# Row sums inverted through DRAM, and the value product of a pair's second half in one piece

## The reference

```python
qf = jnp.concatenate([q_nope, q_pe], axis=-1)        # 128 + 64 wide
kf = jnp.concatenate([k_nope, k_pe], axis=-1)
scores = jnp.einsum('bhnd,bhmd->bhnm', qf, kf) * scale
scores = jnp.where(causal, scores, jnp.finfo(scores.dtype).min)
attn = jax.nn.softmax(scores, axis=-1)
out = jnp.einsum('bhnm,bhmd->bhnd', attn, v)
out = out.transpose(0, 2, 1, 3).reshape(b, n, HEADS * VDIM)
return out @ Wout
```

## Time and profile before

| | |
|---|---|
| median of 3 runs | 1745.24 us (1744.07 to 1745.45) |
| span of the profiled execution | 1743.9 us, its mean granted clock 0.996 |
| TensorE busy | 1690.3 us, 97% |
| VectorE busy | 1237.6 us, 71% |
| ScalarE busy | 982.1 us, 56% |
| GpSimd busy | 572.6 us, 33% |
| preparation, attention loop, feed-forward part | to about 70 us, to about 1243 us, to the end |

### The profile page before, as it was taken

One profiled execution on the slowest core, in us unless ns is written; L12 is line 12 of the kernel. 1 busy time (PEld: TensorE's weight loads), 2 busy tenths in 40 slices (PEclk: granted clock), 3 DMA queues, 4 the chain that ended last, 5 costly groups with the idle time before them and its releaser, 6 DMA issues. The chain is left out here.

```text
span 1743.9 us, 32128 instructions
## 1 busy us (share of the span) xinstructions
PE 1690.3 (97%) x11280; PEld 1384.5 (79%) x11280; DVE 1237.6 (71%) x2858; ACT 982.1 (56%) x2319; POOL 572.6 (33%) x498
## 2 busy tenths in 40 slices
PE   5799999999999999999999999999999999999998
PEld 4677777778777777777777777777699999999998
DVE  6878788778788788787887878877654454555543
ACT  6566666666666666666666666666533333433332
POOL 4553344434443344433344334434401110110100
PEclk9899999999999999999999999999999999999999
DMA  8300000012000003000001100001200000000000
GB/s 285 123 7 7 7 14 7 8 30 76 13 8 7 7 7 103 8 7 7 9 12 49 56 7 14 7 7 42 81 1 25 25 1 25 25 13 13 13 13 13
DMA packets 35868, 51.45 MB, mean 30 GB/s; under 512 B 2368, under 2 KB 26944, under 8 KB 35712
## 3 DMA queue, kind: packets, MB, share of 16 engines
q1 hardware_dynamic: 35712, 49.39, 8.7%
HBM read 35.23 MB, written 14.16 MB: 28 GB/s over the span
## 5 line engine op out<-in xcount | busy, mean ns | idle before, releaser
L1296 ACT ACTIVATE probs<-aps,nmax 128x384 f32<-128x384 f32 (+7 forms) x512 | 378.8, 744 | 215.9 <-DVE nmax L1353 210.1
L1353 DVE CUSTOM_DVE_ANT_0 aps<-aps,mask_row 128x384 f32<-128x384 f32 (+7 forms) x512 | 388.6, 770 | 132.0 <-PE aps L43 125.7
L1222 PE MATMUL aps<-ident,probs 128*128 128x128 f32 x2304 | 329.1, 272 | 0.8 <-ACT probs L1296 0.6
L43 PE MATMUL aps<-kTh,qh 128*128 128x512 f32 (+3 forms) x768 | 293.6, 382 | 8.8 <-POOL ql L1452 3.8
L1222 PEld LDWEIGHTS aps<-ident,probs 128*128 128x128 f32 x2304 | 271.8, 140 | 23.3 <-issue 1.4
L1307 ACT COPY pT<-aps 128x512 f32<-128x512 f32 (+3 forms) x485 | 233.8, 506 | 89.1 <-PE aps L1222 86.2
L43 PE MATMUL aps<-pT,v 128*64 128x512 f32 (+3 forms) x1536 | 268.9, 492 | 0.6 <-ACT pT L1307 0.6
L43 PE MATMUL aps<-kTl,qh 128*128 128x512 f32 (+3 forms) x768 | 257.4, 343 | 0.0
L1445 POOL TENSOR_TENSOR rot<-rot 64x512 f32<-64x512 f32 x128 | 163.4, 1277 | 185.8 <-DVE rot L1367 185.8
L43 PEld LDWEIGHTS aps<-pT,v 128*64 128x64 f32 x1536 | 101.7, 136 | 152.1 <-issue 142.1
L43 PE MATMUL aps<-kTh,ql 128*128 128x512 f32 (+3 forms) x768 | 221.7, 343 | 0.0
(11 more groups left out here) (193 smaller groups left out, 3037.4 us busy)
## 6 DMA issues: line engine op xcount, KB each, us to landing
wqs<-wq_scratch SPq DMA_DIRECT2D x30, 256.0 KB, 2.6
raw_numbers<-in_x SPq DMA_DIRECT2D x8, 512.0 KB, 6.6
acc<-in_x SPq DMA_DIRECT2D x8, 512.0 KB, 3.6
x_scratch<-acc SPq DMA_DIRECT2D x8, 512.0 KB, 3.0
x<-x_scratch SPq DMA_DIRECT2D x8, 512.0 KB, 3.9
out<-x SPq DMA_DIRECT2D x7, 512.0 KB, 2.9
heads<-in_heads SPq DMA_DIRECT2D x4, 640.0 KB, 8.2
wout<-in_Wout SPq DMA_DIRECT2D x4, 512.0 KB, 8.8
```

The source lines that it names most:

```text
L43: return nc.tensor.matmul(out, lhsT, rhs, start=start, stop=stop, skip_group_check=True)
L1222: last = nc.tensor.transpose(tps[:, TS.index(x) % 3, j * P:(j + 1) * P], probs[c][:, c * (pair % 2), a, off:off + P], t.ident[:])
L1296: nc.scalar.activation(probs[c][:, c * (r % 2), a, off:off + w], sps[:, at:at + w], ACT.Exp, bias=nmax[:, c, a, j:j + 1], scale=-1.0, accu ...
L1353: nc.vector.tensor_tensor_reduce(out=s, in0=s, in1=mask[:, N - PW[c][j]:N], scale=-1.0, scalar=3.0e38, op0=ALU.add, op1=ALU.min, accum_out ...
```

## The change

The four transposes L(c), the product REP(c) and the copy LOUT(c) go. INV(c) now writes its eight inverses per token into the first of 32 columns and turns them with VectorE's own transpose, which works on blocks of 32x32: inverse m of tokens 32s to 32s + 31 comes to lie on partition 32s + m. `spread_inverses` on SP stores the four blocks to a DRAM scratch of 8 rows of 128 numbers, waits for them, and loads each head's four rows to 64 partitions of `linv_b`. O(c) waits for these two loads.

PV(1, 0, 4) and PV(1, 4, 4) become PV(1, 0, 8) in the place of the second. `pT` has 16 buffers instead of 12, and a block's buffer is counted on through the bodies. All other jobs keep their order. In body 32 four jobs of GpSimd stand ahead of the loop over its list, which had them behind REP(1). The scratch that the compiler keeps for dynamic DMAs is set to 1024.

```diff
-PT_BUFS = 12
+PT_BUFS = 16
...
-                  T(1, 3, 0), L(1), T(1, 2, 0), Y(0, 0), T(1, 1, 1), S(0, 0, 1), T(1, 2, 1), S(0, 1, 1),
-                  S(0, 1, 3), T(1, 0, 0), S(0, 0, 3), T(1, 7, 0), T(1, 4, 0), Q(1, 0), Q(0, 1), PV(1, 0, 4),
-                  S(1, 1, 2), T(1, 7, 1), T(1, 6, 0), T(1, 5, 1), Q(0, 0), L(0), T(1, 4, 1), T(1, 5, 0),
-                  T(1, 6, 1), S(1, 0, 3), S(1, 0, 0), T(0, 1, 0), PV(1, 4, 4), S(1, 1, 0), T(0, 0, 1),
+                  T(1, 3, 0), T(1, 2, 0), Y(0, 0), T(1, 1, 1), S(0, 0, 1), T(1, 2, 1), S(0, 1, 1),
+                  S(0, 1, 3), T(1, 0, 0), S(0, 0, 3), T(1, 7, 0), T(1, 4, 0), Q(1, 0), Q(0, 1),
+                  S(1, 1, 2), T(1, 7, 1), T(1, 6, 0), T(1, 5, 1), Q(0, 0), T(1, 4, 1), T(1, 5, 0),
+                  T(1, 6, 1), S(1, 0, 3), S(1, 0, 0), T(0, 1, 0), PV(1, 0, 8), S(1, 1, 0), T(0, 0, 1),
...
+        def buffer(x, r):
+            return ((r + 1) * len(TS) + TS.index(x)) % PT_BUFS
...
+            def spread_inverses(c, r):
+                n = nth(c, r)
+                if n > 1:
+                    sp.wait_ge(o_sb, count(L(c), r - 1))
+                sp.wait_ge(l_turned, count(L(c), r))
+                for s in range(4):
+                    sp.dma_start(t.l_dram[c, :, 32 * s:32 * s + 32], linv_t[32 * s:32 * s + 8, c, :]).then_inc(l_kept[c], 16)
+                sp.wait_ge(l_kept[c], KEPT * n)
+                for a in range(2):
+                    row = t.l_dram[c, 4 * a:4 * a + 4].rearrange("m p -> (m p)")
+                    sp.dma_start(linv_b[64 * a:64 * a + 64, c, :], row.partition_broadcast(64)).then_inc(l_sb[c], 16)
...
+            spread_inverses(0, 0)
             for r in range(1, B * PAIRS + 1):
+                spread_inverses(1, r)
                 if r + 1 < B * PAIRS and r % PAIRS != 1 or r == 1:
...
+                if r < LAST - 1:
+                    spread_inverses(0, r)
...
                 def inv_job(x):
                     _, c = x
                     dve.wait_ge(e_done, max(count(y, r + age(x)) for y in SS if y[1] == c))
-                    if exists(L(c), r - 1):
-                        dve.wait_ge(l_rep, count(L(c), r - 1))
-                    nc.vector.reciprocal(linv[:, c], lsum[:, c]).then_inc(l_inv, 1)
+                    if nth(c, r) > 1:
+                        dve.wait_ge(l_kept[c], KEPT * (nth(c, r) - 1))
+                    nc.vector.reciprocal(linv[:, c, 0:8].rearrange("p (a j) -> p a j", a=2), lsum[:, c])\
+                        .then_inc(l_inv, 1)
+                    dve.wait_ge(l_inv, count(L(c), r))
+                    nc.vector.transpose(linv_t[:, c, :], linv[:, c, :]).then_inc(l_turned, 1)
...
-                    dve.wait_ge(l_sb, count(L(c), r))
+                    dve.wait_ge(l_sb[c], 32 * nth(c, r))
```

More of the change, by code:

```diff
@@ L919, in INV @@
             return ("inv", c)
[L921 to L925, removed]
         def O(c):
@@ L976, in attention @@
                         EXP(0, 0, 2), HIGH(1, 0), EXP(0, 0, 3), EXP(1, 1, 1), OUT(0, 1, 0), HIGH(0, 1), EXP(1, 1, 0),
-                        EXP(1, 1, 2), OUT(0, 1, 1), EXP(1, 0, 0), OUT(0, 3, 1), LOUT(0), HIGH(0, 0), EXP(1, 0, 2),
+                        EXP(1, 1, 2), OUT(0, 1, 1), EXP(1, 0, 0), OUT(0, 3, 1), HIGH(0, 0), EXP(1, 0, 2),
                         OUT(0, 3, 0), EXP(1, 0, 3), EXP(1, 1, 3), EXP(1, 0, 1), OHIGH(0)]
-        POOL_FIRST = [ADD(1, 1), LOW(1, 1), ADD(1, 0), LOW(1, 0), ADD(0, 1), REP(0), LOW(0, 1), ADD(0, 0), LOW(0, 0),
+        POOL_FIRST = [ADD(1, 1), LOW(1, 1), ADD(1, 0), LOW(1, 0), ADD(0, 1), LOW(0, 1), ADD(0, 0), LOW(0, 0),
                       OLOW(0)]
@@ L999, in attention @@
                        ACC(1, 1)]
-        SCALAR_LAST = [R(0), R(1), OUT(1, 1, 0), OUT(1, 3, 1), OUT(1, 0, 1), OUT(1, 3, 0), LOUT(1), OUT(1, 2, 0),
+        SCALAR_LAST = [R(0), R(1), OUT(1, 1, 0), OUT(1, 3, 1), OUT(1, 0, 1), OUT(1, 3, 0), OUT(1, 2, 0),
                        OUT(1, 1, 1), OUT(1, 2, 1), OUT(1, 0, 0), OUT(1, 7, 0), OUT(1, 4, 0), R(2), OUT(1, 7, 1),
@@ L1039, in attention @@
             COUNT.update({(name, x, r): n + 1 for n, (x, r) in enumerate(done)})
+        sums = [(L(x[1]), r) for r in BODIES for x in body(VECTOR, VECTOR_FIRST, r) if x[0] == "inv"]
+        COUNT.update({("L", x, r): n + 1 for n, (x, r) in enumerate(sums)})
         def evac(x, r):
@@ L1093, in place, with nth @@
             return P if PW[c][j] == 5 * P else 0
+        KEPT = 64
+        def nth(c, r):
+            return r + age(L(c)) + 1
         @block.sync
         def _(sp):
+            def spread_inverses(c, r):
[9 more added lines that the diff above has]
+                    sp.dma_start(linv_b[64 * a:64 * a + 64, c, :], row.partition_broadcast(64)).then_inc(l_sb[c], 16)
             def load_wq(pair):
@@ L1202, in s_job @@
                     last.then_inc(s_ready, 1)
[L1204 to L1210, removed]
                 def t_job(x):
@@ L1242, in pv_job @@
                             last = mm(nc, ops[64 * a:64 * a + 64, s:QC], t.v32[:, pair // PAIRS % 2, kb, :],
-                                      pT[:, k % PT_BUFS, s:QC], kb == 0, kb == KB[c] - 1)
+                                      pT[:, buffer(TS[k], r), s:QC], kb == 0, kb == KB[c] - 1)
                     last.then_inc(pv_done, 1)
@@ L1269, in mask_job @@
                     mask_products(nc, t, 0, banks[:, 5, :])
-                job = {"q": q_job, "s": s_job, "l": l_job, "t": t_job, "p": pv_job, "y": y_job, "router": router_job,
+                job = {"q": q_job, "s": s_job, "t": t_job, "p": pv_job, "y": y_job, "router": router_job,
                        "mask": mask_job}
@@ L1306, in out_job @@
                         act.wait_ge(pv_done, count(product_of(y), rr))
[L1307 to L1311, removed]
-                    if exists(L(c), r - 1):
-                        act.wait_ge(o_sb, count(L(c), r - 1))
-                    nc.scalar.copy(linv_b[:, c, :], sps[:, slot(L(c), r):slot(L(c), r) + QC]).then_inc(l_sb, 1)
+                    nc.scalar.copy(pT[:, buffer(x, r), s:QC], tps[:, k % 3, s:QC]).then_inc(t_sb["scalar"], 1)
                 def ohigh_job(x):
@@ L1321, in ohigh_job @@
                     nc.scalar.copy(oh[:, c * QC:(c + 1) * QC], o32[:, c, :]).then_inc(o_high, 1)
-                job = {"high": high_job, "exp": exp_job, "out": out_job, "lout": lout_job, "ohigh": ohigh_job}
+                job = {"high": high_job, "exp": exp_job, "out": out_job, "ohigh": ohigh_job}
                 def router_job(x):
@@ L1377, in out_job @@
                         dve.wait_ge(pv_done, count(product_of(y), rr))
-                    nc.vector.tensor_copy(pT[:, k % PT_BUFS, s:QC], tps[:, k % 3, s:QC]).then_inc(t_sb["vector"], 1)
+                    nc.vector.tensor_copy(pT[:, buffer(x, r), s:QC], tps[:, k % 3, s:QC]).then_inc(t_sb["vector"], 1)
                 def inv_job(x):
@@ L1406, in run @@
                 if r == BODIES[0]:
+                    nc.vector.memset(linv[:], 0.0).then_inc(l_cleared, 1)
+                    dve.wait_ge(l_cleared, 1)
                     nc.vector.memset(t.spot_v.tensor[:], 0.0)
@@ L1471, in olow_job @@
                                             ALU.subtract).then_inc(o_low, 1)
-                job = {"add": add_job, "low": low_job, "rep": rep_job, "olow": olow_job}
+                job = {"add": add_job, "low": low_job, "olow": olow_job}
+                if r == LAST:
+                    for n in FIRST_QUAD[2:]:
+                        split_first_quad(nc, t, n)
+                    router_root(nc, t, 1)
+                    for i in range(HT):
+                        router_norm(nc, t, 1, i)
                 for x in body(POOL, POOL_FIRST, r):
@@ L1486, in run @@
                             split_first_quad(nc, t, n)
[L1487 to L1492, removed]
             nc.gpsimd.memset(mask[:, 0:N - P], 0.0).then_inc(mask_cleared, 1)
-            nc.gpsimd.memset(ones[:], 1.0)
             nc.gpsimd.memset(t.minus_half[:], -0.5)
```

46 lines of the change are left out of this document (18 added, 28 removed).

## The result

The changed kernel takes 1826.58 us (median of 4 runs, 1826.23 to 1827.38) against 1745.35; the ratio is 1.0467, 95% interval 1.0453 to 1.0482. It is slower by 81 us. The time lies within the wide range of 1785 to 1835 us, 18 us above the forecast of 1808.4, and it went the way that was forecast. It lies 2.6 us above the forecast's own range of 1793 to 1824.

A forecast was written before the change was run, and what follows sets the result against it. TensorE was taken as the bound, with a VectorE-ScalarE chain level with it; 31 bodies x 2.02 = 62.6, plus 0.6 at the edges, gives span 1807.1 and forecast 1808.4 us; own range 1793 to 1824, wide range 1785 to 1835.

The forecast's parts named there:

- L: Transposes leaving TensorE: L(1) saves 0.43 us a body, L(0), lying inside the chain, is worth nothing on its own.
- The bared chain: ROT(1,0), INV(0), ROT(0,1), MAX(1,1,2), then the exponential lose the product's cover; 7.82 us from Q(1,0) to S(1,0,3), 8.75 before.
- x: Extra time for the turning on VectorE in INV(0): 0.22 us, bounds 0.1 and 0.6.
- The product: Joined value product behind the scores on TensorE: 3.58 + 2.30 - 0.20 = 5.68 us.
- credit of 0.2 for a change of form: Saving on TensorE from joining the two value products: 0.2 us a body, bounds 0 and 0.4.
- OUT(0,1,0) and DRAM: The copy waiting in VectorE's queue for the product, and the inverses' stores and loads on SP: 0 each.
- the way through DRAM: Four stores and two spreading loads on SP with landings: 9.2 us at most, 6.5 with landings half as long; hidden.
- The body: One full attention loop body: 37.99 us against 35.97, +2.02 us.
- rival 2: Clock falls in TensorE's new idle time: 1861 us if in each body, 1826 if in a third; chance 8%.
- if the clock falls within the loop: One of the prediction's signs, in the attention loop, that it is wrong.
- Rival 1: TensorE stays the bound, S(1,0,3) finds its banks free: 1.06 us a body gained, 1712 us; chance 8%.
- rival 3: SP late: weights for Q(0,1) land over 2.5 us behind need; 1839 us at 1 us more; chance 4%.

The follow-up runs named there:

- experiment 2: Changed kernel with the two products of four key blocks and 12 buffers back, row sums still through DRAM: 1732.02 us, ratio 0.9924.
- experiment 1: Kernel before with only the joined product PV(1,0,8) and 16 buffers, row sums as before: 1819.47 us, ratio 1.0425.
- experiment 3: Changed kernel with INV(0) moved behind MAX(1,1,2) in VectorE's list: 1805.31 us, ratio 1.0346.
- experiment 4: Changed kernel with MAX(1,1,2) directly behind ROT(1,0) and INV(0) behind MAX(1,0,0) on VectorE: 1793.14 us, ratio 1.0272.
- experiment 6: Changed kernel with the late product split into PV(1,0,4) and PV(1,4,4) side by side in the same place: 1826.22 us, ratio 1.0464.
- experiment 5: Changed kernel with five unused 128x512 matmuls a body added on TensorE between T(1,6,1) and S(1,0,3): 1812.42 us, ratio 1.0386.
- experiment 8: Two-product kernel with row sums through DRAM, 16 buffers, first product cut into PV(1,0,1) and, behind three T, PV(1,1,3): 1725.02 us, ratio 0.9882.
- experiment 7: Two-product kernel with row sums through DRAM, 16 buffers, two T and S(1,1,2) ahead of PV(1,0,4), T(1,5,1) behind: 1746.41 us, ratio 1.0006.

## Why the prediction was right, point by point

*L.* -0.43 a body for L(1) and nothing for L(0): experiment 2, 35.56 against 35.97.

*The bared chain.* Experiments 1, 3 and 4 show it. One reading of the kernel before was too wide: level with TensorE ran only the part from S(1,1,2) on, since MAX(1,1,2) waited 1.19 us for these scores; the rotations in front of it had that much room and set the time only once the product was gone. From Q(1,0) to S(1,0,3) the forecast had 7.82 us; the row has 658.89 - 651.04 = 7.85. TensorE's idle time was put at 3.1 us in pieces of 0.7, 1.0 and 1.5; it is 2.9 in pieces of 0.49, 0.90 and 1.52.

*x.* Forecast 0.22; the next rotation starts 654.28 - 653.90 = 0.38 behind the reciprocal instead of 0.12, so 0.26. The transpose starts 0.24 us behind the reciprocal that it waits for, where the nearest unwaited successor came 0.12 behind. The 0.12 for x that the prediction drew from the rule of "VectorE: DVE Perf Modes" of the Trainium skill ("The DRAIN you can't avoid") was too low here; the two successors are different instructions, so what the wait alone costs isn't shown.

*The product.* Forecast 5.68, measured 5.74: of the credit of 0.2 for a change of form 0.14 is there. Experiment 6 has it too, with two products side by side: it comes from their standing together and not from their being one.

*OUT(0,1,0) and DRAM.* Both were put at 0. MAX(1,1,0) starts 668.65 - 667.39 = 1.26 us behind the product's end, before it was 632.58 - 631.39 = 1.19. OUT(0,1,0) waited 4.95 us where 4 were forecast, and by experiment 6 that wait costs nothing. The load of the inverses landed after 2.8 us, the stores sooner than allowed for. The lower figure for the way through DRAM, 6.5 us, was added up wrongly: with landings half as long its terms give 6.0. Nothing hangs on it.

*The body.* 37.99 forecast, 38.03 to 38.07 measured.

*What the forecast lacked* is 18.2 us: 8 x 1.55 = 12.4 from falls of the clock in the loop, 2.4 in the last body, where there is one more fall (33.33 us against 30.92; 31.63 in experiment 5, without a fall); the other bodies have 0.04 to 0.08 us more each, and under 1 us each lies at the first body and around the span. The step that failed is the choice between the forecast and rival 2. By the prediction's own signs it was wrong there: "if the clock falls within the loop" was one of them. The price of a fall was near (1.7 us against 1.55), the chance of 8% that it is paid was too low. That the 1826 us for falls in a third of the bodies meet the measured 1826.6 is luck: 8 falls at 1.7 give 1822, and the rest came from the last body and small terms. So the mechanism of the loss and the time of a body without a fall were forecast, and the falls were left out. The reason given against rival 2, that no piece of idle time reaches 2 us, does not hold: in the changed kernel the piece ahead of the fall shown is 1.53 us, with 0.86 and 0.52 in the 7 us before. The page "TensorE: Matmul & The Clock Gate" of the Trainium skill ("HAM oscillation — how this bites in real kernels") describes long waits for DMA data; here waits of 0.5 to 1.5 us for ScalarE close to one another were enough.

*The rivals.* Rival 1 (TensorE stays the bound) fell with experiments 3 and 5, rival 3 (SP late) with the trace and experiment 2. Its kernel without the bared chain exists, though: it is experiment 8.

## What to carry to other kernels

An instruction block on a saturated engine can be worth its place more than its time: before moving or joining it, take it out of the row of queues and see which chain stands behind it, in every queue that the chain passes (experiment 7 failed on ScalarE's, which its theory left out). A wait that is level with the bound shows in no list of waits; look for releasers that end within 0.2 us of the start of what they release. And idle time can cost twice: here the clock fell behind it, and filling it with useless work made the kernel 14 us faster.

## What the runs showed of the hardware that was not expected

- The granted clock fell to 1.2 GHz in 8 of 31 bodies (the changed kernel) and in 9 (experiment 6) with 2.9 us of idle time each in three pieces, in 3 with one piece shorter by 0.3 (experiment 3), and in none with 2.0 us of idle time (experiment 4), with 1.7 us where useless work filled the rest (experiment 5) or with 2.2 us where L(0) stands in it (experiment 1). A fall cost 1.55 us.
- VectorE's transpose of 128x32 takes 0.21 us and starts 0.24 us behind the start of the reciprocal that it waits for.
- Four stores of 1 KB to DRAM in rows of 128 bytes were issued, landed and seen by SP within 2.2 us (2.9 us in the body before the one shown).
- The weights' load of 256 KB takes 3.2 us to landing in the median, going out behind the two spreading loads; in the kernel before and in experiment 1, which have no such loads, it takes 2.6.
